# Second layer of a two-layer graph network: four row buffers, and weighted one-hot rows made column by column

## What is computed

```python
def _L1_gnn_ref(h, norm, weight, gate_weight, src, dst, rel_type):
    all_msg = jnp.einsum('nf,rfo->rno', h, weight)
    msg = all_msg[rel_type, src] * norm
    all_gate = jnp.einsum('nf,rf->rn', h, gate_weight[..., 0])
    gate = jax.nn.sigmoid(all_gate[rel_type, src])[:, None]
    msg = msg * gate
    agg = jax.ops.segment_sum(msg, dst, num_segments=n_nodes)
    return jax.nn.relu(agg)
x = _layernorm(x + _L0_gnn_ref(x, ..., src, dst, edge_type_5, node_type_3), axis=-1)
x = _layernorm(x + _L1_gnn_ref(x, edge_weight1, ..., src, dst, edge_type_16), axis=-1)
```

## Time and profile before

| | |
|---|---|
| median of the runs | 1795.22 us |
| span of the profiled execution | 2218.8 us |
| mean granted clock of PE | 0.814 |
| PE busy | 1448.9 us (65%) |
| DVE busy | 929.2 us (42%) |
| GpSimd busy | 905.9 us (41%) |
| ScalarE busy | 496.8 us (22%) |

### The profile page before, as it was taken

The page is one execution under the profiler, slowest core; times in us unless marked ns, Lnnn a source line. Parts: engine busy times, 40 slices in busy tenths (PEclk is TensorE's granted clock), DMA queues, the critical chain, the costliest instruction groups (busy, mean ns, idle before and its releaser), DMA issues.

```text
span 2218.8 us, 20926 instructions
## 1 busy us (share of the span) xinstructions
PE 1448.9 (65%) x6758; PEld 1177.4 (53%) x6758; DVE 929.2 (42%) x1589; ACT 496.8 (22%) x1056; POOL 905.9 (41%) x906
## 2 busy tenths in 40 slices
PE   4999985676587656777677775679444554454444
PEld 3888874565476545665566554567333333343333
DVE  7334353754465445555464544554132313221321
ACT  2222222232333223323242332334100000000000
POOL 1130003744233432223332333220566776667765
PEclk9999996788788887889878888789676667667667
DMA  5343465645444554434544455443433333333332
GB/s 116 118 124 119 140 216 161 183 147 169 142 138 134 171 158 128 129 122 150 169 150 133 139 162 162 123 136 86 113 90 91 95 104 90 89 89 106 101 89 81
DMA packets 103738, 286.44 MB, mean 129 GB/s; under 512 B 20689, under 2 KB 40308, under 8 KB 100560
## 3 DMA queue, kind: packets, MB, share of 16 engines
q0 software_dynamic: 56064, 169.35, 25.4%
q1 hardware_dynamic: 47642, 116.69, 17.3%
HBM read 189.33 MB, written 96.65 MB: 129 GB/s over the span
## 4 chain that ended last, share of the span: by engine, by line
PE 37%; another core or an unknown queue 30%; DVE 11%; issue 7%; POOL 7%; DMA 4%; ACT 3%; DVEq 0%; ACTq 0%; SPq 0%; POOLq 0%
PE bank L793 9%; PE bank L770 8%; POOL kv L583 7%; PE bank L666 5%; PE bank L728 4%; DMA kv_table<-tstage 3%; PE bank L716 3%; PE bank L672 2%; DVE onehot_r L1277 2%; PE bank L683 2%; DVE kv L1285 1%; DVE onehot_w L1277 1%; PE bank L881 1%; PE bank L690 1%
## 5 line engine op out<-in xcount | busy, mean ns | idle before, releaser
L583 POOL DMA_INDIRECT kv<-kv_table,idx x416 | 417.1, 1003 | 696.1 <-DVE idx L1272 572.9
L583 POOL DMA_INDIRECT kv<-message_table,idx x416 | 451.8, 1086 | 271.9 <-issue 217.3
L881 PE MATMUL bank<-kv,onehot_w 128*121 128x256 f32 x832 | 312.1, 548 | 336.1 <-DMA kv<-message_table,idx 302.7
L881 PEld LDWEIGHTS bank<-kv,onehot_w 128*121 128x121 f32 x832 | 226.0, 279 | 422.2 <-DMA kv<-message_table,idx 205.0
L770 PE MATMUL bank<-wr_r,x1T_r 128*121 128x512 f32 x1248 | 357.3, 430 | 22.1 <-issue 11.7
L770 PEld LDWEIGHTS bank<-wr_r,x1T_r 128*121 128x121 f32 x1248 | 234.1, 199 | 83.3 <-issue 20.1
L1020 ACT ACTIVATE mstage<-bank,gate 121x256 f32<-121x256 f32 x416 | 171.0, 470 | 228.9 <-PE bank L770 134.1
L1425 DVE SCALAR_TENSOR_TENSOR z<-bank,xb 121x256 f32<-121x256 f32 x26 | 11.0, 423 | 473.1 <-remote 445.7
L793 PE MATMUL bank<-kv,onehot_r 128*121 128x264 f32 x832 | 202.1, 391 | 0.0
L784 PE MATMUL bank<-ident,carry 8*128 8x8 f32 x26 | 6.3, 240 | 276.9 <-DVE carry L1354 266.7
L793 PEld LDWEIGHTS bank<-kv,onehot_r 128*121 128x121 f32 x832 | 150.1, 185 | 28.8
(11 more groups left out here) (138 smaller groups left out, 1709.7 us busy)
## 6 DMA issues: line engine op xcount, KB each, us to landing
message_table<-mstage SPq DMA_DIRECT2D x104, 484.0 KB
kv_table<-tstage SPq DMA_DIRECT2D x26, 1210.0 KB
kv<-kv_table,idx POOLq DMA_INDIRECT x416
kv<-message_table,idx POOLq DMA_INDIRECT x416
query_table<-qstage_r SPq DMA_DIRECT2D x26, 242.0 KB
qb_r<-query_table SPq DMA_DIRECT2D x26, 242.0 KB
kv<-in_Wr POOLq DMA_DIRECT2D x2, 2048.0 KB, 12.5
xb<-in_x SPq DMA_DIRECT2D x26, 121.0 KB
```

The lines of the kernel that those rows point to most:

```text
L583: pool.indirect_dma_start(kv[:, par, u, 0:width], None, table, bass.IndirectOffsetOnAxis(ap=idx[:, par, u:u + 1], axis=0)).then_inc(landed ...
L881: last = mm(bank[r.par][:NODES, 0:C], onehot_w[:, r.par, u, :], kv[:, r.par, u, 0:C], start=(u == 0), stop=(u == U - 1))
```

## The change

The rows of the second layer go to four buffers, `mrows`, which take the place of both halves of `kv`; PE's sums go to four PSUM banks. A class `Turn` numbers the rounds by four. `n = 2` is the first turn, so that 26 rounds end with a whole group of four: two rounds are written out, then four, a loop of five iterations of four, and four more. GpSimd's indirect DMAs take their row numbers straight from `rows`, so that the copies into `idx` fall away; all 416 are written out, and a round waits for PE's sum of four rounds before. DVE makes one-hot rows two rounds ahead of the one that it finishes, and makes them with 16 operations of [128, 121], each of which compares with one column of `dstl` and multiplies by one column of `norms`. The rest is names: `row_index` and `make_onehot` now serve the first layer alone.

```diff
+LB = 4
+QUADS = (ROUNDS - 2) // LB
...
+class Turn:
+    def __init__(self, eng, i, q):
+        self.eng, self.i, self.q, self.par = eng, i, q, q % 2
+        self.number = i * LB + (q - 2)
+        self.done = i * LB + (q - 1)
+        self.again = i * LB + (q - 5)
+        self.used = i * 128 + (128 if q >= 2 else 0)
+    @property
+    def refills(self):
+        return not (isinstance(self.i, int) and self.number < LB)
...
+    def ahead(self):
+        return Turn(self.eng, self.i, self.q + 2) if self.q < 2 else Turn(self.eng, self.i + 1, self.q - 2)
...
+def turns(eng, body):
+    for q in (2, 3):
+        body(Turn(eng, 0, q))
+    for q in range(LB):
+        body(Turn(eng, 1, q))
+    with eng.Fori(2, QUADS) as i:
+        for q in range(LB):
+            body(Turn(eng, i, q))
+    for q in range(LB):
+        body(Turn(eng, QUADS, q))
...
-            onehot_w = lsb("onehot_w", [P, 2, U, NODES])
+            onehot_w = lsb("onehot_w", [P, LB, U, NODES])
+            mrows = kv[:, :, :, :].rearrange("p b u c -> p (b u c)")[:, 0:LB * U * C].rearrange(
+                "p (b u c) -> p b u c", b=LB, u=U)
...
+        b_l = (bank[0], bank[1], bank[2], bank[4])
...
-            with pool.Fori(1, ROUNDS // 2 + 1) as pair:
-                gather(pair, mtab, C, l_idx, l_landed)
+            def gather_messages(r):
+
+                if r.refills:
+                    pool.wait_ge(l_agg, r.again)
+                for u in range(U):
+                    pool.indirect_dma_start(mrows[:, r.q, u, :], None, mtab,
+                                            bass.IndirectOffsetOnAxis(ap=rows[:, 1, r.number, u:u + 1], axis=0)
+                                            ).then_inc(l_landed[r.q][u * 2 // U], 16)
+            for n in range(2, ROUNDS + 2):
+                gather_messages(Turn(pool, n // LB, n % LB))
...
             def l1(r):
-                wait(pe, l_z, r.before)
+                if r.refills:
+                    pe.wait_ge(l_z, r.again)
                 pe.wait_ge(l_oh, r.done)
                 for u in range(U):
                     if u % (U // 2) == 0:
-                        pe.wait_ge(l_landed[r.par][u * 2 // U], r.loads(U // 2))
-                    last = mm(bank[r.par][:NODES, 0:C], onehot_w[:, r.par, u, :], kv[:, r.par, u, 0:C],
+                        pe.wait_ge(l_landed[r.q][u * 2 // U], r.used)
+                    last = mm(b_l[r.q][:NODES, 0:C], onehot_w[:, r.q, u, :], mrows[:, r.q, u, :],
                               start=(u == 0), stop=(u == U - 1))
                 last.then_inc(l_agg, 1)
             pe.wait_ge(qe_used[1], ROUNDS * QB)
-            rounds(pe, l1)
+            turns(pe, l1)
...
+            def weigh_onehot(r):
+
+                if r.refills:
+                    dve.wait_ge(l_agg, r.again)
+                j = bass.ds(r.number, 1)
+                for u in range(U):
+                    last = v.tensor_scalar(onehot_w[:, r.q, u, :], iota_n[:, :], dstl[:, j, u], norms[:, j, u],
+                                           ALU.is_equal, ALU.mult)
+                last.then_inc(l_oh, 1)
+
             def l1(r):
-                wait(dve, l_agg, r.before)
-                make_onehot(r, l_oh0, onehot_w)
-                dve.wait_ge(l_oh0, r.done)
-                w = norms[:, bass.ds(r.number, 1), :].rearrange("p j u -> p (j u)").unsqueeze(2).broadcast_to([P, U, NODES])
-                o = onehot_w[:, r.par, :, :]
-                v.tensor_tensor(o, o, w, ALU.mult).then_inc(l_oh, 1)
-                if not r.first:
-                    finish(r.last())
-                    if not r.final:
-                        row_index(r.next(), 1, l_idx)
-
-            row_index(Round(dve, 0, 0), 1, l_idx)
-            row_index(Round(dve, 0, 1), 1, l_idx)
+                if not (isinstance(r.i, int) and r.number + 2 >= ROUNDS):
+                    weigh_onehot(r.ahead())
+                finish(r)
+
             dve.wait_ge(x1_stored, 16 * ROUNDS)
             dve.wait_ge(m_filled[1], ROUNDS * MB)
-            rounds(dve, l1)
-            finish(Round(dve, LAST, 1))
+            for q in (2, 3):
+                weigh_onehot(Turn(dve, 0, q))
+            turns(dve, l1)
```

More of the change, by code:

```diff
@@ L116, in next, with loads, stores_before @@
         return Round(self.eng, self.i, 1) if self.par == 0 else Round(self.eng, self.i + 1, 0)
+class Turn:
[8 more added lines that the diff above has]
+        return not (isinstance(self.i, int) and self.number < LB)
+    def loads(self, n):
+        return self.i * (32 * n) + 16 * n * (self.q // 2)
+    def stores_before(self):
+        return self.i * (16 * LB) + 16 * (self.q - 2)
+    def ahead(self):
[10 more added lines that the diff above has]
+        body(Turn(eng, QUADS, q))
 def settle(eng, sem):
@@ L309, in build @@
         x1_stored = sem("x1_stored")
-        l_idx, l_oh0, l_oh, l_agg = sems("l_idx", 2), sem("l_oh0"), sem("l_oh"), sem("l_agg")
-        l_landed = [sems(f"l_landed{p}_", 2) for p in range(2)]
+        l_oh, l_agg = sem("l_oh"), sem("l_agg")
+        l_landed = [sems(f"l_landed{q}_", 2) for q in range(LB)]
         l_x = sems("l_x", 2)
@@ L573, in _, with gather @@
             pool.memset(carry[:, 1, P:P + 1], -BIG).then_inc(carry_ends, 1)
-            def gather(pair, table, width, indices, landed):
+            def gather(pair):
                 for par in range(2):
                     settle(pool, const_ready)
-                    if isinstance(pair, int) and par == 1 and table is ktab:
+                    if isinstance(pair, int) and par == 1:
                         pool.wait_ge(wr_low, HALVES)
-                    pool.wait_ge(indices[par], pair)
+                    pool.wait_ge(idx_ready[par], pair)
                     for u in range(U):
-                        pool.indirect_dma_start(kv[:, par, u, 0:width], None, table,
+                        pool.indirect_dma_start(kv[:, par, u, 0:2 * C], None, ktab,
                                                 bass.IndirectOffsetOnAxis(ap=idx[:, par, u:u + 1], axis=0)
-                                                ).then_inc(landed[par][u * len(landed[par]) // U], 16)
-            gather(1, ktab, 2 * C, idx_ready, kv_landed)
+                                                ).then_inc(kv_landed[par][u // GU], 16)
+            gather(1)
             with pool.Fori(2, ROUNDS // 2 + 1) as pair:
-                gather(pair, ktab, 2 * C, idx_ready, kv_landed)
+                gather(pair)
             for b in range(PARTS):
@@ L1268, in _, with row_index, make_onehot @@
             v.memset(den[:, :], 1.0).then_inc(tables_over, 1)
[L1270 to L1275, removed]
+            def row_index(r):
+                v.tensor_copy(idx[:, r.par, :], rows[:, 0, bass.ds(r.number, 1), :].rearrange("p j u -> p (j u)")
+                              ).then_inc(idx_ready[r.par], 1)
+            def make_onehot(r):
                 d = dstl[:, bass.ds(r.number, 1), :].rearrange("p j u -> p (j u)").unsqueeze(2).broadcast_to([P, U, NODES])
-                v.tensor_tensor(to[:, r.par, :, :], iota_n[:, :].unsqueeze(1).broadcast_to([P, U, NODES]), d,
-                                ALU.is_equal).then_inc(signal, 1)
+                v.tensor_tensor(onehot_r[:, r.par, :, :], iota_n[:, :].unsqueeze(1).broadcast_to([P, U, NODES]), d,
+                                ALU.is_equal).then_inc(oh_ready, 1)
             def score(r, g):
@@ L1385, in l0 @@
                     if not r.final:
-                        row_index(r.next(), 0, idx_ready)
+                        row_index(r.next())
                 score(r, 2)
@@ L1392, in l0 @@
                 if not r.final:
-                    make_onehot(r.next(), oh_ready, onehot_r)
+                    make_onehot(r.next())
                 softmax_across(r)
@@ L1400, in l0 @@
                     keep_x1T_low(f)
[L1402 to L1404 removed]
+            row_index(Round(dve, 0, 0))
+            row_index(Round(dve, 0, 1))
+            make_onehot(Round(dve, 0, 0))
             dve.wait_ge(carry_ends, 1)
```

5 lines of the change are left out of this document (1 added, 4 removed).

## The result

The changed kernel takes 1746.2 us (median of 4 runs, 1742.67 to 1750.01), the kernel before 1793.7 us (4 runs, 1787.31 to 1796.57): a ratio of 0.9736, 95% interval 0.9717 to 0.9755, so 47.5 us less. The forecast was 1747 us.

What follows compares the result with a forecast made beforehand. GpSimd's issue of gathers was taken to bound the second layer. Held gathers gain 58.3 us, the train costs 10.4, index waits give nothing in timed runs: 47.9 us off 1795.2 gives 1747 us, range 1728 to 1792.

Steps and rivals of the forecast that it cites:

- its floor: Second layer, GpSimd: 416 gathers issued back to back at 1.25 us each, 520 us.
- The 58.3 us: Second-layer gathers lasting longer beside DVE's two whole-tensor operations, 2.24 us a round; all of it to be gained.
- The middle bound of 10.4 us: Cost of the 16-operation DVE train to second-layer gathers: 0.11 us each for 3.6 gathers, 0.4 us a round.
- The lower bound: Least cost of the DVE train to gathers: nothing, as one gather beside a two-scalar operation took its plain 0.95 us.
- Rivals 2 and 3: Rival 2: each meeting costs three operations, 1779 us, chance 0.10; rival 3: train holds the port without gap, 1838 us, 0.10.
- The forecast of the profiled span, 2116: Whole profiled execution: 58.3 - 10.4 + 54.6 = 102.5 us less than 2218.8 us.
- a timed gain near half of the profiled one: Sign that the prediction is right: 47.9 us gained in timed runs against 102.5 us in the profiled execution.
- rival 1: GpSimd's second-layer index waits are real in timed runs too, giving 1693 us; chance 0.07.
- The profile after should show none of it in GpSimd's idle time: Second layer: four buffers cover PE lateness of 17 us, so GpSimd shows no wait from it.
- my 47.9: Whole timed gain in us: 58.3 of held gathers less 10.4 for the train.
- the 578: Second layer of the kernel before in a timed run: 632.9 - 54.6 us of gathers back to back, 22.2 us a round.
- tail unchanged: End of the second layer, behind the last gathers: the change was taken to leave its time as it was.

Runs made afterwards that it cites:

- columns_alone: The kernel before with only the 16 column operations, keeping two row buffers, index copies and loops: 2212.4 us, ratio 0.9933 against the kernel before.
- psum_operand: The changed kernel with two whole-tensor operations again, one input of each read from PSUM: 2194.45 us, ratio 0.9845 against the kernel before.
- buffers_alone: The changed kernel with the two whole-tensor operations put back in place of the 16 column operations: 2211.49 us, ratio 0.9922 against the kernel before.
- Control: The kernel before, unchanged, timed and profiled once more on a slow chip: 2230.23 us, ratio 1.0003.
- changed: The changed kernel as it is, run again on the second slow chip: 2190.59 us, ratio 0.9864 against the kernel before.
- light_before: The kernel before with 14 of each second-layer round's 16 columns left out of PE's sum: 2123.32 us, ratio 0.9779 against the kernel before.
- light_changed: The changed kernel with 14 of each second-layer round's 16 columns left out of PE's sum: 2143.21 us, ratio 0.9882 against the kernel before.
- light_columns: The kernel before with the 16 column operations, and 14 of 16 columns left out of PE's second-layer sum: 2123.56 us, ratio 0.9814 against the kernel before.

## Why the prediction was right, and where it was wrong

**Right: the bound and its floor.** GpSimd's issue of gathers sets the second layer: 521.0 us measured, 520 said, with only 0.30 us between gathers as its list of signs asked, a mean of 949 ns within 0.95 to 1.0, and trains of 4.17 us where about 4.5 was said (0.26 us an operation, not 0.28).

**Right: what held the gathers.** The 58.3 us were put on the two operations with two inputs in SBUF. columns_alone and psum_operand remove it, each by another edit, and buffers_alone keeps it.

**Mis-sized: the train's cost.** The middle bound of 10.4 us came from a train of the same operation, where DMA issues of GpSimd were 0.03 to 0.24 us longer. The gathers lost 394.6 - 393.5 = 1.1 us. By my own count in the trace, 73 gathers of after start while DVE is in a train, and take 0.96 us in the mean; of 102 that start while DVE is in one of the first layer's operations with two inputs in SBUF (L1408, L1310), 76 are held up, to 1.8 and 1.9 us in the mean. The lower bound, from the earlier trace rows, was the truth: a direct DMA issue was a poor stand-in for an indirect one, and the nearer row was the gather that I had.

**Rivals 2 and 3** fall with it: 4.17 us of train stand beside three gathers of 0.95, 0.98 and 0.95 us. The Trainium skill's rule ("SBUF — State Buffer", SBUF: two separate sides) that a DVE operation in a 2-port mode holds the pair of ports as well doesn't come out here, if the 16 run in such a mode. No row names the mode. My estimate from rows speaks for it: 414 ns for 256 columns with two scalars (L1469 in after) and 335 in the median for 121 are about 0.6 ns a column, where a two-tensor operation takes 2170 / 1936 = 1.1. That they hold nothing is shown; why is not.

**Half wrong: how the profiled execution stands to the timed ones.** That PE's lateness is in the profile and not in the timed runs was right, and so was its size: 364 us were put on the first layer, and after's first layer is 368 us shorter (1204 against 836). Wrong was to take the profile before and the profile after as of one kind. Control showed the lateness beside runs that all take 2223 us or more, so it isn't a matter of profiled against timed. The forecast of the profiled span, 2116, fails with it (1747.7 measured with the runs of the result, 2185.4 for the same kernel on the second chip), and the sign "a timed gain near half of the profiled one" can't be read. On slow chips rival 1 is half right: the index waits are real there and buffers_alone removes them, for 0.8 and 0.5% of the time. "The profile after should show none of it in GpSimd's idle time" also holds only where PE is on time; in changed 68.8 us stay, behind a sum that is up to 59 us late, not the 17 of the earlier trace rows.

**Right number, one part open.** The gathers gained 58.3 - 1.1 = 57.2 us, the time 47.5 (44 to 51 by the interval). That my 47.9 hit it is luck: its train term was 9 us too dear, so something else costs about 10, and the two cancel. One candidate is the 58.3 itself, taken from a profile with index waits in it. light_before is the only trace of the old operations on two row buffers without such waits, and there the holding is 52.5 us, 6 less. An estimate from the times points the same way: 521.0 + 47.5 = 568.5 us from first to last for the kernel before, less than the 578 that I took, which leaves 48.5 us above the floor and no room for index waits. Another is the end. The prediction took the tail as unchanged; from the end of the last gather to the end of the span is 22.2 us in after (1747.7 - 1725.5), 17.4 in the profile before (2218.8 - 2201.4), which could be 5 of them, but the second is from an execution with late signals. Over all profiles this end lasts 12.8 to 18.0 us with two row buffers and 16.5 to 35.8 with four, so "tail unchanged" is doubtful in itself. The stage ahead of the first layer, 8 us longer in after, is a third candidate, but the profiles scatter there by as much whatever the kernel. No profile of the kernel before in the surroundings of the result exists, so this stays open; so does the split into halves there. That the buffers bring nothing where PE is on time is argued (no wait left to remove), not measured.

## What to carry to other kernels

Before reasoning on a gap between a profile and timed runs, ask whether both come from one chip in one condition: stages that the change doesn't touch tell it at once (1204 against 836 us here), and prices of single operations carry over where spans don't. While GpSimd issues indirect DMAs, a DVE operation should have at most one tensor in SBUF; move the other to PSUM or make it a scalar, even at the same busy time. Many small instructions are as good as two large ones only where no slow stretches stand between them: if the two-operand form is what hurts, one operand in PSUM removes it without them (0.9845 on one slow chip against 0.9864 on another, overlapping).

## What the runs showed of the hardware

Beside a DVE operation with two inputs in SBUF (2.17 us), an indirect DMA issued by GpSimd takes up to 2951 ns instead of 946; with one of the two inputs in PSUM, or as a train of one-tensor operations, it takes 947 to 949 in the mean.

The same kernel takes 1794 us in the runs of the result and 2172 to 2228 on three chips. On these, an engine that by the profile lacks nothing begins for tens of microseconds one instruction in 0.70 or 1.40 us, seen on PE (25 matmuls in 60 us at a granted clock of 0.50) and on DVE (one operation of 0.34 us in 1.40); the profile names such time "issue" or, for whoever waits, "remote". Signals are late beside it, by up to 59 us from PE to DVE in changed and up to 10.1 us from DVE to itself in light_changed. With less work on PE such stretches did not end, and stood on DVE; whether they moved there, or the third chip has them there anyway, wasn't traced. Whether it is a late supply of instructions, register updates of up to 1.4 us, or a throttle beyond the granted clock, no run here tells; it stays open. So does what held light_changed's gathers for 19.7 us, which light_columns' train did not.
